# The last additions of an AdaLN transformer pair: three of eight chunks scaled by ScalarE and added by GpSimd, five by VectorE

## The chip, the cores and the metric

One core of one Trainium2 chip runs the whole program. The metric is the device time in microseconds of one launch, taken as the median of several runs. DVE is VectorE, ACT is ScalarE, POOL is GpSimd, PE is TensorE, SP is SyncE (which here only issues transfers and waits).

## What is computed

Two transformer layers with adaptive layer norm over 16 sequences of 256 tokens of width 128 (4096 tokens). Each layer has an attention part and a mixture of experts, and both add their result to the residual `x`, scaled by a gate that depends on the sequence. The change touches the very last line of this:

```python
x = L0_attn_x                                      # (16, 256, 128)
...                                                # layer 0: attention, experts
h = _layernorm(x) * (1 + ca) + sa                  # layer 1
x = x + ga * _L1_attn_ref(h, ...)
h = _layernorm(x) * (1 + cb) + sb
x = x + gb * _L1_ffn_ref(h, ...)                   # gb: one value per sequence and feature
return x
# inside _L1_ffn_ref, 7 routed experts and a shared one:
return ALPHA * top1_val[..., None] * routed + shared
```

## The kernel before

The residual lies in on-chip memory for the whole run as `X`, features on the 128 partitions and the 4096 tokens along the free axis. It is worked in eight chunks (`NCH`) of 512 tokens (`CH`), each of two sequences (`BPC`) of 256 tokens (`SEQ`).

The routed experts work on tokens sorted by expert. Each sorted tile of 128 tokens goes through PE (L677 transposes it, L686 and L693 are the two input products, L703 the output product), is weighted by ACT (L1028), and is sent back to its tokens' rows in the DRAM tensor `token_rows` by an indirect transfer that POOL issues (L1668). The last shared-expert products (L637, L639, L646) follow; DVE adds them with `add_shared`.

What is left then is the return of the routed results:

- SP, in `returned(1)` (L307 to L318), waits for all indirect transfers (L312) and issues eight loads of 256 KB, one a chunk, from `token_rows` into `N` (L316). The last of them waits for the last product that still reads its part of `N`.
- PE, in `turn_back(1, k)` (L727), waits for the load of chunk k, and from k = 2 on for DVE to have finished chunk k - 2, then transposes four 128x128 pieces into PSUM bank 6 or 7 (L734).
- DVE, in `add_routed(1, k)` (L1487), does two `gated` instructions a chunk (L1337), one for each sequence, because the gate `gab` is a column of its own for each sequence: `X = PS * gab + X`, 128x256 each.
- SP, at L325 to L328, goes through the chunks in order, waits for chunk t to be added (L326) and issues its store of 256 KB to `out` (L327), and then waits for all stores to land.

ACT and POOL have nothing to do in this stretch. ACT's queue ends with the SiLU of the last shared products, POOL's with its last `send`. The buffers `sqb` and `rsb` (four slots of 128x512 each) serve the experts in slots 0 and 1; slots 2 and 3 are free there. `va_ones` and `wo_zero` are semaphores of a few fills that POOL does at the start of the program.

Of the kernel before, what the change touches and what calls it, by code (L numbers as in the profile page):

```python
# [14 lines left out]
ALU = mybir.AluOpType  # L15
ACT = mybir.ActivationFunctionType
AX_X = mybir.AxisListType.X

P = 128
BATCH, SEQ, D = 16, 256, 128  # L20
TOK = BATCH * SEQ
CH = 512
NCH = TOK // CH
BPC = CH // SEQ
# [17 lines left out]
def adaln_kernel(nc, a):  # L42
    ctx = ExitStack()
    with ctx:
# [3 lines left out]
        def sem(name):  # L48
            return ctx.enter_context(nc.semaphore(name))


        X = sb("X", [P, TOK])
        H = sb("H", [P, TILES * ROW])
        N = sb("N", [P, TOK])
# [4 lines left out]
        ident = sb("ident", [P, P])  # L59
# [34 lines left out]
        gab = sb("gab", [P, 4, BATCH])  # L94
# [3 lines left out]
        wo1 = sb("wo1", [P, 2, D])  # L98
# [16 lines left out]
        sqb = sb("sqb", [P, 4, CH])  # L115
        rsb = sb("rsb", [P, 4, CH])
# [41 lines left out]

        PS = ctx.enter_context(nc.psum_tensor("PS", [P, 8, CH], FP32))

        C_QB, C_KB, C_OUTB, C_GA, C_BA, C_G1, C_B1, C_G2, C_B2, C_INL, C_FB2 = range(11)

        def col(n):
# [20 lines left out]
        RS = [{n: sem(f"r{l}_{n}") for n in (  # L184
            "xt", "logits", "s_gate", "onehot", "counts", "step", "pos",
            "dispatched", "s_up", "s_silu", "s_hidden", "s_sum", "s_x",
            "back", "x")} for l in range(2)]
# [4 lines left out]
        chunk_in = [sem(f"chunk_in{n}") for n in range(NCH)]  # L192
        r_fill, r_fix = sem("r_fill"), sem("r_fix")
        st_out = sem("st_out")
        va_ones, wo_zero = sem("va_ones"), sem("wo_zero")

        block = ctx.enter_context(nc.Block())

# [45 lines left out]
        def _(sp):  # L244
# [14 lines left out]
            for dst, src in ((wqkv, a["wqkv"]), (vb, a["vb"]), (qmask, a["qmask"]),  # L259
                             (ident, a["ident"]), (identb, a["identb"]), (maskqk, a["maskqk"]),  # L260
                             (maskkq, a["maskkq"])):
                sp.dma_start(dst[...], src).then_inc(ld_a, 16)
            sp.wait_ge(va_ones, 1)
            for head in range(HEADS0):
                p = 32 * (head // 4) + HD0 * (head % 2)
                sp.dma_start(wout[p:p + HD0, head % 4 // 2, :], a["wout"][head * HD0:(head + 1) * HD0, :]).then_inc(ld_a, 16)
# [6 lines left out]
            for dst, src in ((wpv[:, 0:HEADS1 * DEPTH], a["wp"]), (wpv[:, HEADS1 * DEPTH:], a["wv1"]), (bp[:, :, :], a["bp"]),  # L273
                             (prefix[:, :], a["prefix"])):
                sp.dma_start(dst, src).then_inc(ld_l1, 16)
            sp.wait_ge(wo_zero, 1)
            for head in range(HEADS1):
                p = 32 * (head % 4)
                sp.dma_start(wo1[p:p + HD1, head // 4, :], a["wo1"][head * HD1:(head + 1) * HD1, :]).then_inc(ld_l1, 16)
# [43 lines left out]
            tiles(1)  # L323
            returned(1)
            for t in range(NCH):  # L325
                sp.wait_ge(RS[1]["x"], t + 1)  # L326
                sp.dma_start(a["out"][:, t * CH:(t + 1) * CH], X[:, t * CH:(t + 1) * CH]).then_inc(st_out, 16)  # L327
            sp.wait_ge(st_out, 16 * NCH)  # L328

# [2 lines left out]
        def _(pe):  # L332
# [159 lines left out]
            for t in range(A_STEPS):  # L492
                b, u, v = t // 8, t % 8, t - A_LAG
# [233 lines left out]
            def turn_back(l, k):  # L727

                q = RS[l]
                pe.wait_ge(chunk_in[k], 16 * l + 32)  # L730
                if k >= 2:
                    pe.wait_ge(q["x"], k - 1)
                for n in range(4):
                    m = nc.tensor.transpose(PS[:, 6 + k % 2, n * P:(n + 1) * P], N[:, k * CH + n * P:k * CH + (n + 1) * P],  # L734
                                            ident[:, :])
                m.then_inc(q["back"], 1)
# [15 lines left out]
            pe.wait_ge(RS[0]["s_x"], NCH)  # L752
            ln(LN_MODA1, X, residual_ready)
            pe.wait_ge(ld_l1, LD_L1)
            pe.wait_ge(va_ones, 7)

            def project_zv(b):
                pe.wait_ge(ln_out, LNO + 8 * LN_MODA1 + b // BPC + 1)
# [94 lines left out]

            pe.wait_ge(ld_m1, 64)
            moe(dict(MOE[1], ready_pe=lambda k: pe.wait_ge(b_x, 2 * k + 2)))
            for k in range(NCH):
                turn_back(1, k)


        @block.scalar  # L860
        def _(act):
# [242 lines left out]
            invert_sums1(BATCH - 1)  # L1104

            moe(MOE[1])


        @block.vector
        def _(dve):  # L1110
# [130 lines left out]
                    dve.wait_ge(a_pj, b)  # L1241
                nc.vector.tensor_tensor(ao[:, :], av[:, :], rec[:, :], ALU.mult).then_inc(a_on, 1)

            dve.wait_ge(va_ones, 6)
            dve.wait_ge(mod_step, 10)
            for t in range(A_STEPS):
                b, u = t // 8, t % 8
# [239 lines left out]
            def add_routed(l, k):  # L1487
                dve.wait_ge(RS[l]["back"], k + 1)
                if k == NCH - 1:
                    dve.wait_ge(RS[l]["s_x"], NCH)  # L1490
                for b in range(BPC):
                    m = gated(l, k * BPC + b, PS[:, 6 + k % 2, b * SEQ:(b + 1) * SEQ])
                m.then_inc(RS[l]["x"], 1)
# [93 lines left out]

            dve.wait_ge(b_x, BATCH)
            moe(MOE[1])
            for k in range(NCH):  # L1590
                add_routed(1, k)


        @block.gpsimd
        def _(pool):
# [29 lines left out]
                                                ALU.is_ge, 0.0, base=0, channel_multiplier=-1)  # L1625
                m.then_inc(b_cut, 1)

            nc.gpsimd.memset(wo1[:, :, :], 0.0).then_inc(wo_zero, 1)
            nc.gpsimd.memset(wout[:, :, :], 0.0).then_inc(va_ones, 1)
            nc.gpsimd.memset(region[:, 0:3 * VAW], 0.0).then_inc(va_ones, 1)  # L1630
            nc.gpsimd.memset(mxs[:, :, :], 0.0).then_inc(va_ones, 1)
            pool.wait_ge(va_ones, 3)
            for n in range(3):
                nc.gpsimd.memset(region[:, n * VAW:n * VAW + 2 * HEADS0 * 32].rearrange("p (k c) -> p k c", c=32)[:, :, 24:32],
                                 1.0).then_inc(va_ones, 1)
# [20 lines left out]
            def moe(c):  # L1656
                l, q = c["l"], RS[c["l"]]
                pool.wait_ge(q["pos"], 1)
                pool.wait_ge(r_fill, 48)
                for n in range(TILES):  # L1660
                    pool.wait_ge(q["s_hidden"], n * 7 // 8 + 3 if l else min(n * 2 // 3 + 1, NCH * c["NH"] + 2 - LATE_AT[l]))
                    nc.gpsimd.indirect_dma_start(sorted_rows[l][:, :], bass.IndirectOffsetOnAxis(pos[:, n:n + 1], 0),  # L1662
                                                 rows[l][:, n, :], None).then_inc(q["dispatched"], 16)

                def send(k):
                    r = k % RING
                    pool.wait_ge(q["y"], l * SLOTS + k + 1)
                    nc.gpsimd.indirect_dma_start(  # L1668
                        token_rows[l][:, :], bass.IndirectOffsetOnAxis(slot_in[:, r, D:D + 1].bitcast(mybir.dt.int32), 0),
                        slot_out[:, k % OUTS, :], None).then_inc(q["sent"][r], 16)  # L1670

                for k in range(SLOTS_AT[l]):
                    send(k)
# [12 lines left out]
            for n in range(4 * BATCH):  # L1686
                cut1(n)
            moe(MOE[1])


# [75 lines left out]
```

## Time and profile before

| | us |
|---|---|
| median of 3 runs | 1017.04 |
| lowest and highest run | 1012.84, 1019.17 |
| the profiled execution, its own time | 1007.75 |
| its span, from the first to the last instruction | 1006.0 |
| granted TensorE clock over the span, of full speed | 0.978 |

The profile shows one execution. Its span is 1.75 us shorter than its own time, and its own time is 9.3 us (0.9%) below the median of the three timed runs. PE is busy for 93% of the span, and the chain of work that ended last runs over PE for 81% of it; DVE is busy for 62%, ACT for 55%, POOL for 46%. Positions in microseconds below are from the start of the span. The stretch that the change touches lies between 996 and 1006.

### The profile page before, as it was taken

How to read it: one execution, taken by the hardware profiler on the slowest of the kernel's cores; microseconds unless marked ns; L12 is line 12 of the kernel's file. 1: busy time of each engine (PE TensorE's matmuls, PEld its weight loads, DVE VectorE, ACT ScalarE, POOL GpSimd, SP SyncE). 2: the span in 40 equal slices, each digit the busy share in tenths (PEclk: the TensorE clock that was granted, in tenths of full speed). 3: DMA queues.
4: the chain of work that ended last, by engine and by line, in shares of the span. 5: the costliest groups of instructions: out<-in, count | busy, mean ns of one | idle time of the engine just before them, and what ended most of it. 6: DMA issues, size and time to landing. Idle time of an engine off the chain costs nothing.

```text
span 1006.0 us, 21539 instructions
## 1 busy us (share of the span) xinstructions
PE 932.9 (93%) x7391; PEld 600.5 (60%) x7391; DVE 621.9 (62%) x2056; ACT 554.8 (55%) x1075; POOL 460.2 (46%) x697
## 2 busy tenths in 40 slices
PE   8999999999989989999996798889997999999997
PEld 3566777777654223334642796456664644499995
DVE  4788888888824975872553454578772653344444
ACT  5536676766666554574521474567875622255551
POOL 1146777777741955640056464344552043323331
PEclk9999999999999997999999899999997999999999
DMA  6720000000001000031011335000000000121115
GB/s 216 240 72 13 8 13 13 10 10 13 13 20 76 0 0 1 0 121 47 1 35 45 82 96 192 13 2 1 3 1 1 1 30 29 34 61 49 50 30 178
DMA packets 38329, 45.82 MB, mean 46 GB/s; under 512 B 7840, under 2 KB 31648, under 8 KB 37360
## 3 DMA queue, kind: packets, MB, share of 16 engines
q1 hardware_dynamic: 33712, 35.13, 11.6%
q0 software_dynamic: 4512, 9.32, 2.8%
q8 instruction: 62, 1.02, 0.4%
q14 instruction: 43, 0.35, 0.1%
HBM read 31.19 MB, written 18.69 MB: 50 GB/s over the span
## 4 chain that ended last, share of the span: by engine, by line
PE 81%; ACT 6%; DVE 6%; issue 3%; POOL 2%; DMA 1%; SPq 0%; DVEq 0%; ACTq 0%; POOLq 0%
PE PS L686 5%; PE PS L703 5%; PE PS L693 5%; PE PS L444 5%; PE PS L486 5%; PE PS L340 4%; PE PS L637 4%; PE PS L639 4%; PE PS L646 4%; PE PS L457 4%; PE PS L349 3%; PE PS L546 2%; PE PS L437 2%; PE PS L813 2%; PE PS L794 2%
## 5 line engine op out<-in xcount | busy, mean ns | idle before, releaser
L922 ACT ACTIVATE pw<-PS 128x384 f32<-128x384 f32 x256 | 111.6, 488 | 71.2 <-PE PS L466 68.5
L1602 POOL TENSOR_SCALAR_AFFINE_SELECT pw<-pw 128x256 f32<-128x256 f32 x256 | 104.6, 432 | 75.3 <-ACT pw L922 73.1
L1200 DVE CUSTOM_DVE_ANT_0 PS<-PS,above 128x256 f32<-128x256 f32 x256 | 115.9, 453 | 31.4 <-PE PS L437 31.2
L1668 POOL DMA_INDIRECT token_rows<-xnb,slot_in x77 | 73.8, 958 | 104.3 <-ACT xnb L1028 104.3
L1654 POOL TENSOR_TENSOR XS<-XS,N 128x512 f32<-128x512 f32 x64 | 81.1, 1289 | 57.1 <-DVE N L1278 34.6
L444 PE MATMUL PS<-kf,qm 32*128 32x256 f32 x512 | 103.4, 426 | 0.5 <-POOL qm L1611 0.5
L1454 DVE TENSOR_TENSOR rsb<-sqb,PS 128x256 f32<-128x256 f32 (+1 forms) x77 | 42.6, 553 | 84.6 <-PE PS L693 84.0
L1202 DVE CUSTOM_DVE_ANT_0 PS<-PS,above 128x128 f32<-128x128 f32 x256 | 84.6, 330 | 0.0
L1624 POOL TENSOR_SCALAR_AFFINE_SELECT pw<-pw 128x256 f32<-128x256 f32 x128 | 55.9, 471 | 59.8 <-ACT pw L1073 59.8
L1611 POOL TENSOR_SCALAR qm<-qs,qmask 128x256 f32<-128x256 f32 x64 | 59.5, 931 | 44.7 <-ACT kf L903 44.7
L1011 ACT ACTIVATE sqb<-PS 128x512 f32<-128x512 f32 x48 | 28.7, 597 | 89.2 <-PE PS L637 89.2
L469 PE MATMUL PS<-qm,kf 32*128 32x256 f32 x512 | 76.3, 374 | 0.0
L1362 DVE TENSOR_TENSOR rsb<-sqb,PS 128x512 f32<-128x512 f32 x48 | 32.9, 687 | 70.1 <-PE PS L639 69.9
L1172 DVE TENSOR_TENSOR xnb<-PS,rsb 128x512 f32<-128x512 f32 x56 | 38.7, 691 | 58.7 <-ACT rsb L888 49.7
L1662 POOL DMA_INDIRECT sorted_rows<-H,pos x32 | 30.9, 965 | 80.7 <-DVE pos L1434 66.8
L1662 POOL DMA_INDIRECT sorted_rows<-region,pos x32 | 30.7, 959 | 80.3 <-DVE pos L1434 48.8
L686 PE MATMUL PS<-xnb,pw 128*128 128x128 f32 x460 | 64.8, 277 | 0.0
L693 PE MATMUL PS<-xnb,pw 128*128 128x128 f32 x460 | 64.4, 276 | 0.0
L970 ACT ACTIVATE PS<-PS,cols 128x512 f32<-128x512 f32 x64 | 42.2, 662 | 39.3 <-PE PS L546 24.1
L437 PE MATMUL PS<-kf,qm 32*128 32x128 f32 x512 | 62.4, 270 | 0.0
L546 PE MATMUL PS<-N,wxs 128*128 128x512 f32 x112 | 60.1, 623 | 2.0 <-DVE N L1287 0.4
L437 PEld LDWEIGHTS PS<-kf,qm 32*128 32x128 f32 x512 | 60.8, 185 | 0.8
(214 smaller groups left out, 2363.4 us busy)
## 6 DMA issues: line engine op xcount, KB each, us to landing
sorted_rows<-empty_rows_dram SPq DMA_DIRECT2D x2, 2535.0 KB, 14.7
slot_in<-sorted_rows SPq DMA_DIRECT2D x77, 65.0 KB, 1.9
N<-token_rows SPq DMA_DIRECT2D x16, 256.0 KB, 4.6
X<-xT_dram SPq DMA_DIRECT2D x8, 256.0 KB, 5.6
token_rows<-empty_rows_dram SPq DMA_DIRECT2D x1, 2048.0 KB, 24.9
ATT<-gate_dram SPq DMA_DIRECT2D x1, 2048.0 KB
XS<-down_dram SPq DMA_DIRECT2D x1, 2048.0 KB
H<-up_dram SPq DMA_DIRECT2D x1, 2048.0 KB
```

What stands on the lines that cost most here:

```text
L437: nc.tensor.matmul(PS[:, bank, SEQ:SEQ + P], qm[r, b % 3, g, 0:P], kf[r, b % 3, 0:P], start=True, stop=True).then_inc(a_s, 1)
L444: nc.tensor.matmul(PS[:, bank, 0:SEQ], qm[r, b % 3, g, P:SEQ], kf[r, b % 3, :], start=True, stop=True)
L469: m = nc.tensor.matmul(PS[:, bank, 0:SEQ], kf[r, b % 3, 0:P], qm[r, b % 3, g, :], start=False, stop=True, skip_group_check=True)
L546: nc.tensor.matmul(PS[:, k, :], wxs[:, :], V[:, s], start=False, stop=True, skip_group_check=True).then_inc(i_p, 1)
L686: m = nc.tensor.matmul(PS[:, b, n * P:(n + 1) * P], wgate[:, b, n * P:(n + 1) * P], xnb[:, b, 0:P], start=True, stop=True)
L693: m = nc.tensor.matmul(PS[:, 2 + b, n * P:(n + 1) * P], wup[:, b, n * P:(n + 1) * P], xnb[:, b, 0:P], start=True, stop=True)
L922: nc.scalar.activation(pw[:, w % 2, j + n, :], PS[:, A_PST + (2 * v + n) % 3, 0:3 * P], ACT.Exp).then_inc(a_p, 1)
L1200: nc.vector.tensor_tensor_reduce(x[:, 0:SEQ], x[:, 0:SEQ], above[:, :], 1.0, -3e38, ALU.add, ALU.max, mx[:, t // 8 % 2, 1, j, g:g + 1])
L1202: nc.vector.tensor_tensor_reduce(x[:, SEQ:SEQ + P], x[:, SEQ:SEQ + P], above[:, P:SEQ], 1.0, -3e38, ALU.add, ALU.max, mx[:, t // 8 % 2, 0, ...
L1602: m = nc.gpsimd.affine_select(x[:, :, SEQ * k:SEQ * k + P], x[:, :, SEQ * k:SEQ * k + P], [[0, 2], [1, P]], ALU.is_ge, 0.0, base=0, channe ...
L1654: nc.gpsimd.tensor_tensor(XS[:, s], XS[:, s], V[:, s], ALU.add).then_inc(i_x, 1)
L1668: nc.gpsimd.indirect_dma_start(token_rows[l][:, :], bass.IndirectOffsetOnAxis(slot_in[:, r, D:D + 1].bitcast(mybir.dt.int32), 0), slot_out ...
```

## The change

Of the eight last chunks, 1, 3 and 5 (`SCALED`) no longer go through DVE. ACT reads their transposed values from PSUM, scales them by the gate column and writes them into free slots of `sqb` and `rsb`; POOL adds them to `X`. DVE does chunks 0, 2, 4, 6 and 7 (`ADDED`) as before. PE's transposes go on in the order of the chunks, but alternate between banks 7 and 3 for the scaled ones and between banks 6 and 4 for the others, so a bank is taken again after two chunks of its own path. SP's stores stay in the order of the chunks; for a scaled chunk they wait on a new semaphore `x_added`, two counts a chunk. `add_routed(1, ...)` and `turn_back(1, ...)` are no longer called; for layer 0 both stay. At the start of the program `wo_zero` is folded into `va_ones`, whose counts move up by one.

```diff
+        SCALED, ADDED = (1, 3, 5), (0, 2, 4, 6, 7)
+        scaled = [sqb[:, 2, :], sqb[:, 3, :], rsb[:, 2, :]]
...
-        va_ones, wo_zero = sem("va_ones"), sem("wo_zero")
+        va_ones = sem("va_ones")
+        x_scaled, x_added = sem("x_scaled"), sem("x_added")
...
-            sp.wait_ge(va_ones, 1)
+            sp.wait_ge(va_ones, 2)
...
-            sp.wait_ge(wo_zero, 1)
+            sp.wait_ge(va_ones, 1)
...
             for t in range(NCH):
-                sp.wait_ge(RS[1]["x"], t + 1)
+                if t in SCALED:
+                    sp.wait_ge(x_added, 2 * SCALED.index(t) + 2)
+                else:
+                    sp.wait_ge(RS[1]["x"], ADDED.index(t) + 1)
                 sp.dma_start(a["out"][:, t * CH:(t + 1) * CH], X[:, t * CH:(t + 1) * CH]).then_inc(st_out, 16)
...
+            def turn_last(k):
+
+                pe.wait_ge(chunk_in[k], 48)
+                if k in SCALED:
+                    i, bank = SCALED.index(k), 7 if SCALED.index(k) % 2 == 0 else 3
+                    if i >= 2:
+                        pe.wait_ge(x_scaled, 2 * i - 2)
+                else:
+                    i, bank = ADDED.index(k), 6 if ADDED.index(k) % 2 == 0 else 4
+                    if i >= 2:
+                        pe.wait_ge(RS[1]["x"], i - 1)
+                for n in range(4):
+                    m = nc.tensor.transpose(PS[:, bank, n * P:(n + 1) * P], N[:, k * CH + n * P:k * CH + (n + 1) * P],
+                                            ident[:, :])
+                m.then_inc(RS[1]["back"], 1)
+
             for k in range(NCH):
-                turn_back(1, k)
+                turn_last(k)
...
             moe(MOE[1])
+            for i, k in enumerate(SCALED):
+                act.wait_ge(RS[1]["back"], k + 1)
+                for b in range(BPC):
+                    n = k * BPC + b
+                    nc.scalar.activation(scaled[i][:, b * SEQ:(b + 1) * SEQ], PS[:, 7 if i % 2 == 0 else 3, b * SEQ:(b + 1) * SEQ],
+                                         ACT.Copy, scale=gab[:, 3, n:n + 1]).then_inc(x_scaled, 1)
...
             moe(MOE[1])
-            for k in range(NCH):
-                add_routed(1, k)
+            for i, k in enumerate(ADDED):
+                dve.wait_ge(RS[1]["back"], k + 1)
+                if k == NCH - 1:
+                    dve.wait_ge(RS[1]["s_x"], NCH)
+                for b in range(BPC):
+                    m = gated(1, k * BPC + b, PS[:, 6 if i % 2 == 0 else 4, b * SEQ:(b + 1) * SEQ])
+                m.then_inc(RS[1]["x"], 1)
...
             moe(MOE[1])
+            pool.wait_ge(RS[1]["s_x"], NCH - 1)
+            for i, k in enumerate(SCALED):
+                for b in range(BPC):
+                    s = slice((k * BPC + b) * SEQ, (k * BPC + b + 1) * SEQ)
+                    pool.wait_ge(x_scaled, i * BPC + b + 1)
+                    nc.gpsimd.tensor_tensor(X[:, s], X[:, s], scaled[i][:, b * SEQ:(b + 1) * SEQ], ALU.add).then_inc(x_added, 1)
```

The waits on `va_ones` that other engines have at the start (PE's 7, DVE's 6, POOL's 3) become 8, 7 and 4.

## Rows read from the trace of the kernel before

**Rows 1.** The chain that ended last, its end: start us, us, what

```profile
996.00 1.67 DVE X L1337 x4
997.67 0.14 issue
997.81 0.64 PE PS L734 x4
...
1002.25 0.87 DVE X L1337 x2
1003.12 0.39 DVEq L44
```

**Rows 2.** Timeline, 960 to 1006: start us, us, engine line what [idle before <-releaser]

```profile
995.80 1.04 PE L734 MATMUL PS<-ident,N 128*128 128x128 f32 x8
...
996.00 7.51 DVE L1337 SCALAR_TENSOR_TENSOR X<-PS,gab,X 128x256 f32<-128x256 f32 x18 [1.22 <-PE PS L646]
```

**Rows 3.** L327, the stores: the first alone, then the last alone

```profile
L327 SPq DMA_DIRECT2D out_dram<-X x1: 350/350/350, 997.7 to 997.7; - x1
...
DMA to landing us min/median/max: 3.2/3.2/3.2
...
L327 SPq DMA_DIRECT2D out_dram<-X x1: 332/332/332, 1003.5 to 1003.5; - x1
...
DMA to landing us min/median/max: 2.0/2.0/2.0
```

**Rows 4.** L316, the loads, each alone: chunks 5, 6 and 7

```profile
L316 SPq DMA_DIRECT2D N<-token_rows x1: 518/518/518, 993.6 to 993.6; - x1
...
DMA to landing us min/median/max: 5.2/5.2/5.2
...
L316 SPq DMA_DIRECT2D N<-token_rows x1: 1187/1187/1187, 994.2 to 994.2; - x1
...
DMA to landing us min/median/max: 5.5/5.5/5.5
...
L316 SPq DMA_DIRECT2D N<-token_rows x1: 709/709/709, 995.4 to 995.4; - x1
...
DMA to landing us min/median/max: 5.0/5.0/5.0
```

**Rows 5.** Windows: length, PE, PEld, DVE, ACT, POOL busy, PEclk, DMA share, GB/s

```profile
1000.00:1001.00 1.00, 0.75 (x6) 0.42 (x4) 0.97 (x4) 0.00 (x0) 0.00 (x0) 1.00 1.05 402
...
1002.00:1003.00 1.00, 0.60 (x4) 0.36 (x4) 1.00 (x3) 0.00 (x0) 0.00 (x0) 1.00 0.99 375
1003.00:1004.00 1.00, 0.00 (x0) 0.00 (x0) 0.51 (x2) 0.00 (x0) 0.00 (x0) 1.00 0.90 344
1004.00:1005.00 1.00, 0.00 (x0) 0.00 (x0) 0.00 (x0) 0.00 (x0) 0.00 (x0) 1.00 0.94 350
```

**Rows 6.** Groups by shape: line engine op, out<-in, count | busy us, mean ns | idle

```profile
L942 ACT ACTIVATE ATT<-PS,cols 128x256 f32<-128x256 f32 x16 | 7.6, 474 | 4.3 <-PE PS L425 4.3
...
L1616 POOL TENSOR_TENSOR H<-H,ATT 128x256 f32<-128x256 f32 x16 | 11.6, 722 | 6.2 <-ACT ATT L942 6.2
```

**Rows 7.** Timeline, 430 to 446, VectorE and GpSimd: additions beside two kinds of VectorE work

```profile
436.85 1.27 POOL L1654 TENSOR_TENSOR XS<-XS,N 128x512 f32<-128x512 f32 x1 [0.45 <-DVE N L1287]
437.26 0.70 DVE L1278 SCALAR_TENSOR_TENSOR PS<-XS,PS 128x512 f32<-128x512 f32 x1 [0.49 <-ACT PS L970]
...
438.59 0.68 DVE L1293 SCALAR_TENSOR_TENSOR H<-XS,H 128x512 f32<-128x512 f32 x1
438.75 1.65 POOL L1654 TENSOR_TENSOR XS<-XS,N 128x512 f32<-128x512 f32 x1 [0.64 <-DVE N L1287]
```

**Rows 8.** The same end of layer 0: windows (as rows 5), then the timeline

```profile
628.00:630.00 2.00, 1.68 (x7) 1.25 (x7) 1.24 (x4) 0.00 (x0) 0.00 (x0) 0.50 1.04 264
...
628.72 1.09 PE L734 MATMUL PS<-ident,N 128*128 128x128 f32 x4 [0.32 <-DMA N<-token_rows]
```

More of the change, by code:

```diff
@@ L754, in _ @@
             pe.wait_ge(ld_l1, LD_L1)
-            pe.wait_ge(va_ones, 7)
+            pe.wait_ge(va_ones, 8)
             def project_zv(b):
@@ L1242, in normalise @@
                 nc.vector.tensor_tensor(ao[:, :], av[:, :], rec[:, :], ALU.mult).then_inc(a_on, 1)
-            dve.wait_ge(va_ones, 6)
+            dve.wait_ge(va_ones, 7)
             dve.wait_ge(mod_step, 10)
@@ L1626, in cut1 @@
                 m.then_inc(b_cut, 1)
-            nc.gpsimd.memset(wo1[:, :, :], 0.0).then_inc(wo_zero, 1)
+            nc.gpsimd.memset(wo1[:, :, :], 0.0).then_inc(va_ones, 1)
             nc.gpsimd.memset(wout[:, :, :], 0.0).then_inc(va_ones, 1)
@@ L1631, in _ @@
             nc.gpsimd.memset(mxs[:, :, :], 0.0).then_inc(va_ones, 1)
-            pool.wait_ge(va_ones, 3)
+            pool.wait_ge(va_ones, 4)
             for n in range(3):
```

## The prediction

> **What bounds the kernel now.** PE bounds nearly all of the span, but the change leaves that part alone, so the reading begins at its end. I read the chain that ended last first. From 996.00 on it goes back and forth between DVE's additions (L1337) and PE's transposes (L734), until DVE ends at 1003.12 + 0.39 = 1003.51 [rows 1]. The timeline then shows DVE without a pause: 18 additions fill 7.51 us, 0.417 us each [rows 2]. Two of them are the last shared ones and sixteen the routed ones, 0.83 us a chunk. So far DVE looks like the limit of this stretch, and three chunks less would be worth 3 x 0.83 = 2.5 us.
>
> The third view says otherwise. The end of the span isn't the end of DVE but the landing of the last store: it is issued at 1003.5 and lands 2.0 us later, at 1005.5, and the span ends 0.5 us after that [rows 3]. The first store, issued at 997.7, took 3.2 us and landed at 1000.9 [rows 3]. A store that needs 2.0 us by itself and takes 3.2 us stood in a queue. From the first landing to the last it is 1005.5 - 1000.9 = 4.6 us for seven more chunks, 0.66 us each. A chunk is 512 x 128 x 4 bytes = 262 KB, and at the 344 to 402 GB/s that the windows show [rows 5] it takes 0.65 to 0.76 us. The share of the transfer engines that is busy stays between 0.90 and 1.05 from 1000 to 1005 [rows 5]. So the stores already follow each other about as fast as the transfers run; DVE only keeps just ahead of them. The loads are the third term. Chunks 5, 6 and 7 are issued at 993.6, 994.2 and 995.4 and land at 998.8, 999.7 and 1000.4 [rows 4], so no engine can add chunk 7 before about 1000.5.
>
> **The change part by part.** I follow each chunk through the new order, with the landings of before.
>
> *PE.* Chunks 0 and 1 are transposed by 995.80 + 1.04 = 996.84, as before [rows 2]. Chunk 2 no longer waits for DVE, since it has bank 4. Four transposes take 0.64 us [rows 1]. With the loads and banks as they are, chunk 2 ends at about 997.4, 3 at 997.95, 4 at 998.6 (its bank is free at 997.67), 5 at 998.8 + 0.65 = 999.5, 6 at 999.7 + 0.7 = 1000.4 and 7 at 1000.4 + 0.7 = 1001.1. Nothing is queued behind these on PE.
>
> *DVE.* The two shared additions and chunk 0 end at 996.00 + 1.67 = 997.67 as before [rows 1]. Chunk 2 ends at 998.5, chunk 4 runs from 998.6 to 999.5. Then DVE waits for a load: chunk 6 from 1000.45 to 1001.3, chunk 7 to 1002.15. DVE drops six instructions, 6 x 0.417 = 2.5 us, but its end moves only from 1003.51 to 1002.15, by 1.36 us, because 0.95 us of the saving becomes a wait for the load of chunk 6 and the rest is the wait ahead of chunk 4 and rounding.
>
> *ACT.* It gets six scaled copies of 128x256 from PSUM. The nearest row, also out of PSUM and with a column as operand, has 474 ns [rows 6], 0.95 us a chunk at most. ACT scales chunk 1 from 996.9 to 997.8, chunk 3 from 998.0 to 998.9, chunk 5 from 999.6 to 1000.5. It sits idle in between. The form itself, Copy with a scale column, runs in the same part of the program (L1028), so I count no table load. If one were needed after all, it would push POOL's chain back, which has 0.4 us of slack (below).
>
> *POOL.* It gets six additions of 128x256 at 722 ns [rows 6], 4.33 us. The first can start when the first half of chunk 1 is scaled, at 997.4. Back to back they end at 998.85 (chunk 1), 1000.3 (chunk 3) and 1001.75 (chunk 5); for chunk 5 the scaled half is ready at 1000.1, so the chain never waits for ACT. The waits that stand on POOL's queue hold nothing else up, because nothing stands behind them.
>
> *SP.* Stores leave in order, and one issue takes 0.33 to 0.35 us [rows 3]. Store 0 goes at 997.7 as before, 1 waits for POOL until 998.9 (before it went some 0.8 us after store 0), 2 goes at 999.25, 3 at 1000.35, 4 at 1000.7, 5 at 1001.8, 6 at 1002.15, 7 at 1002.5. Store 2, whose data is ready at 998.5, is held for 0.75 us behind store 1; that is the price of the fixed order.
>
> *The sum.* The last issue moves from 1003.5 to 1002.5, a gain of 1.0 us at the engine side. At the transfer side the same eight chunks have to go out. The first lands at 1000.9 as before. At 0.66 us a chunk the seventh after it lands at 1000.9 + 4.6 = 1005.5; each store's own earliest landing (issue + 2.0) is checked against that: 1 at 1000.9 against 1001.6, 3 at 1002.35 against 1002.9, 5 at 1003.8 against 1004.2, 7 at 1004.5 against 1005.5. No store is late for its place in the queue, so the transfers end where they did. In the last three microseconds of before the share was 0.99, 0.90 and 0.94 [rows 5], so 0.17 us of idle time could be closed. The term I take is 0.1 us faster. Its bounds: 0.4 us faster, if the seven chunks go at the 402 GB/s of one window [rows 5] less what the loads had of it, about 0.60 us each; and 0.3 us slower, if late stores 1 and 2 leave the transfers with a hole once the loads are done.
>
> The renumbered semaphores at the start cost nothing: the same fills stand in the same order on POOL. Without that cover the wait would be one fill, well under 1 us.
>
> **May POOL and DVE add at the same time?** The rows show both answers. POOL's 128x512 addition took 1.27 us beside L1278, which reads one operand from PSUM and one from on-chip memory, and 1.65 us beside L1293, which reads two from on-chip memory [rows 7], 0.38 us more. The new neighbour, L1337, reads PSUM, `X` and a gate column, so it resembles L1278. I take 0.72 us. The other bound is an addition that each time waits out a whole DVE one, 0.72 + 0.42 = 1.14 us. By the Trainium skill (SBUF — State Buffer, "Who interferes with whom") a VectorE instruction with at most one input in SBUF, outside the two-port modes, doesn't contend with GpSimd, while one with two holds up a GpSimd instruction that reads there. The trace agrees with both halves (1.27 and 1.65 us), and by that rule the sum stays as it is.
>
> **The rivals.**
>
> *The transfers give the gain free.* If a store at the end isn't held by those before it, the last one lands 2.0 us after its issue, at 1004.5, and the kernel is 1.0 us faster. For it: the last store of before took only 2.0 us [rows 3]. Against it: that one came after a share of 0.90 [rows 5], while now stores 5, 6 and 7 come within 0.7 us. The Trainium skill (DMA: Bandwidth & Descriptors, "Anatomy of one DMA") fits one transfer at about 2.0 us plus its bytes at 436 GB/s; as an estimate by that page the last store would land 2.6 us after its issue, at 1005.1, 0.4 us faster, a result inside the forecast's own bounds. The trace differs for a store, 2.0 us with the data in it [rows 3].
>
> *POOL's chain is too slow.* Store 5 keeps its place as long as it is issued by 1005.5 - 2 x 0.66 - 2.0 = 1002.2; the sum has 1001.8. So the chain has 0.4 us of slack, and from (1002.2 - 997.4) / 6 = 0.80 us an addition on it decides. At 1.14 us for the four that run beside DVE and 0.72 us for two, POOL ends at 997.4 + 6.0 = 1003.4, stores 5 to 7 land by 1003.4 + 2.0 + 1.3 = 1006.7, and the kernel is 1.2 us slower; at 1.14 us for all six it ends at 1004.2 and the kernel is 2.0 us slower.
>
> *PE's clock halves in the new gaps.* In layer 0, where PE waited for these loads, the granted clock was 0.50 and four transposes took 1.09 us [rows 8], 0.45 us more than 0.64. Then chunk 7 is added by about 1002.7 and its store leaves at 1002.7; its place in the queue asks for 1003.5. That costs nothing.
>
> **How the numbers follow.** I give the forecast (the transfers decide, 0.4 faster to 0.3 slower) 0.60, the free gain 0.18, POOL's chain 0.22. The sum was made in the profiled execution: span 1006.0 - 0.1 = 1005.9. Added to the median of the runs shown, 1017.04 - 0.1 gives 1016.9. All cases lie between 1.0 us faster and 2.0 us slower, at most 0.2% of the kernel; about 1% is what a measurement of this kernel can tell from no change. The range is therefore that of the measurement: runs of the same kernel lay between 1012.84 and 1019.17, and the profiled one at 1007.75. With the cases at either end of the runs, 1012.84 - 1.0 = 1011.8 and 1019.17 + 2.0 = 1021.2; a median of runs seldom falls at the upper end, while one execution lay below the lower, so I take 1011.5 to 1020.5. Faster or slower by over 1% can only come from such scatter: 0.02 each.
>
> **What would show it.** The last store is issued near 1002.5 less any shift of the stretch, but takes about 3.0 us to land instead of 2.0. DVE sits idle for some 0.9 us ahead of chunk 6, released by PE and behind it the load. POOL's six additions stand back to back at 0.72 us. The share of the transfers stays near 1.0 from chunk 0's store to the end. The forecast is wrong if the last store lands 2.0 us after its issue, if POOL's additions are over 0.80 us, or if ACT loads a table.

## The result, and the profile after

| | us |
|---|---|
| changed kernel, median of 9 runs | 1022.29 (1020.55 to 1025.9) |
| kernel before, median of 9 runs | 1016.25 (1012.84 to 1019.17) |
| ratio, with its 95% interval | 1.0052 (1.0033 to 1.0071) |
| profiled execution: own time, span | 1021.06, 1019.3 |

The change costs about 5.3 us (0.0052 x 1016.25; by the interval 3.4 to 7.2). That is within 1%, as forecast, but the time lies above the range (1011.5 to 1020.5), and the loss is clear of the noise.

The spans of the two profiled executions differ by 13.3 us. To see what of that belongs to the change, a landmark is needed: the start of the last shared product (L646 before, L653 after). It is the last PE instruction that doesn't depend on the returned tokens. The rows give the first and the last start of these products, before and then after.

```profile
L646 PE MATMUL PS<-rsb,XS x64: 592/592/697, 807.2 to 995.4; 128*128 128x512 f32 x64
```

```profile
L653 PE MATMUL PS<-rsb,XS x64: 592/592/697, 813.8 to 1003.7; 128*128 128x512 f32 x64
```

Up to the landmark the profiled executions are 8.3 us apart, in code that is the same in both but for the counts of the fills at the start. From there to the end it takes 1006.0 - 995.4 = 10.6 us before and 1019.3 - 1003.7 = 15.6 us after. Only these 5.0 us match the 5.3 us of the timed runs; the 8.3 us are the scatter of single executions (the profiled one of before was itself 8.5 us under its median). They arise in layer 0, between 560 and 620 us, where PE stands idle now and then in one execution and not in the other. The windows from 580 to 600 us show it (length, then PE, PEld, DVE, ACT and POOL busy, clock, transfer share, GB/s): before, after, and the first kernel of the experiments below, whose code up to the landmark is that of the changed kernel.

```profile
580.00:600.00 20.00, 20.00 (x182) 20.00 (x181) 11.52 (x42) 14.50 (x43) 13.24 (x14) 1.00 0.36 95
```

```profile
580.00:600.00 20.00, 17.82 (x149) 16.73 (x148) 9.33 (x34) 11.47 (x35) 10.70 (x12) 1.00 0.28 78
```

```profile
580.00:600.00 20.00, 20.00 (x182) 20.00 (x181) 11.21 (x42) 14.61 (x42) 13.16 (x14) 1.00 0.36 97
```

What makes one execution take this stretch more slowly is open; the change isn't it, since the third kernel has the changed code there. All positions below with a **t** count from the landmark.

The timeline of the changed kernel shows the new order at work (start, us, engine, line, what, and in brackets the idle time before):

```profile
1005.17 0.84 ACT L1134 ACTIVATE sqb<-PS,gab 128x256 f32<-128x256 f32 x2 [3.11 <-PE PS L875]
...
1005.80 2.79 POOL L1728 TENSOR_TENSOR X<-X,sqb 128x256 f32<-128x256 f32 x4 [7.88 <-ACT sqb L1134]
1005.99 5.45 SPq L334 DMA_DIRECT2D out_dram<-X  x8
...
1007.24 0.88 DVE L1366 SCALAR_TENSOR_TENSOR X<-PS,gab,X 128x256 f32<-128x256 f32 x2 [0.50 <-PE PS L875]
...
1008.12 0.84 ACT L1134 ACTIVATE rsb<-PS,gab 128x256 f32<-128x256 f32 x2 [0.95 <-PE PS L875]
...
1008.68 1.41 POOL L1728 TENSOR_TENSOR X<-X,rsb 128x256 f32<-128x256 f32 x2
1008.94 1.66 DVE L1366 SCALAR_TENSOR_TENSOR X<-PS,gab,X 128x256 f32<-128x256 f32 x4 [0.82 <-PE PS L875]
```

The bracket after POOL's first row is its idle time between its last send and its first addition, 7.88 us. POOL's last addition ends at 1008.68 + 1.41 = 1010.09, DVE's at 1010.60. The last store is issued at t = 7.3, against 8.1 before [rows 3], and lands 2.9 us later, at 1013.9:

```profile
L334 SPq DMA_DIRECT2D out_dram<-X x1: 443/443/443, 1011.0 to 1011.0; - x1
...
DMA to landing us min/median/max: 2.9/2.9/2.9
```

So the output is complete at t = 10.2, and it was complete at t = 1005.5 - 995.4 = 10.1 before [rows 3]. Up to here nothing is gained and nothing is lost. But the program goes on for 5.4 us more, where it took 0.5 us before. The windows of this time show no engine at work, and only the end of the last store:

```profile
1013.00:1015.00 2.00, 0.00 (x0) 0.00 (x0) 0.00 (x0) 0.00 (x0) 0.00 (x0) 0.50 0.07 28
1015.00:1017.00 2.00, 0.00 (x0) 0.00 (x0) 0.00 (x0) 0.00 (x0) 0.00 (x0) 0.50 0.00 0
```

The waits of SP's queue name something at the closing line of the program (L44), put down to PE for want of a better name. Before:

```profile
SPq L44 <- DMA out_dram<-X: 1.7, 1, 1.7
...
SPq L44 <- PEq L44: 0.2, 1, 0.2
```

After:

```profile
SPq L44 <- PEq L44: 5.2, 1, 5.2
SPq L44 <- DMA out_dram<-X: 2.5, 1, 2.5
```

Asked for all instructions of line L44, the trace shows the closing barrier: each engine has a DRAIN and then signals. The drains of ACT, PE and DVE end within 0.1 us of those engines' last work (DVE's after the change at 1010.67, its work at 1010.60). POOL's doesn't. Of before:

```profile
L44 POOLq DRAIN  x1: 10175/10175/10175, 988.4 to 988.4; - x1
...
L44 DVEq DRAIN  x1: 914/914/914, 1002.7 to 1002.7; - x1
...
L44 SPq DRAIN  x1: 7/7/7, 1005.8 to 1005.8; - x1
```

Of after:

```profile
L44 POOLq EVENT_SEMAPHORE  x2: 17/17/17, 1019.1 to 1019.2; - x2
...
L44 PEldq DRAIN  x1: 700/700/700, 1009.0 to 1009.0; - x1
L44 POOLq DRAIN  x1: 10082/10082/10082, 1009.0 to 1009.0; - x1
...
L44 SPq DRAIN  x1: 7/7/7, 1014.1 to 1014.1; - x1
```

POOL's drain is recorded from the time when nothing else is left on its queue, while its last instructions still run, and takes 10 us. Before, it ended at 998.6, 9.0 us after POOL's last send (989.6); the additions and stores went on until 1005.5 beside it, so it cost nothing. After, it ends at 1019.08, again 9.0 us after POOL's last instruction (1010.09), and now only the closing signals come after it. So POOL's queue didn't end with its last send, nor did POOL have nothing to do in this stretch, as was taken ahead of the prediction: its drain stood behind the send.

### The profile page after: what moved, and what is told of

Read it like the earlier page. It is cut to its first block, busy times and chain, and to the rows that moved or that the text cites. A ratio compares the mean times of both kernels' runs of the same rounds, so it can differ in the third digit from the quotient of the medians.

```text
span 1019.3 us, 21544 instructions
## 1 busy us (share of the span) xinstructions
PE 934.6 (92%) x7391; PEld 601.0 (59%) x7391; DVE 619.3 (61%) x2050; ACT 555.9 (55%) x1081; POOL 465.7 (46%) x703
## 3 DMA queue, kind: packets, MB, share of 16 engines
q1 hardware_dynamic: 33712, 35.13, 11.3%
## 4 chain that ended last, share of the span: by engine, by line
PE 78%; ACT 6%; DVE 6%; issue 4%; DMA 2%; POOL 2%; SPq 1%; DVEq 0%; ACTq 0%; POOLq 0%
PE PS L710 6%; PE PS L451 5%; PE PS L493 5%; PE PS L693 5%; PE PS L700 5%; PE PS L347 4%; PE PS L464 4%; PE PS L644 3%; PE PS L646 3%; PE PS L653 3%; PE PS L356 3%; PE PS L553 2%; PE PS L444 2%; PE PS L820 2%; PE PS L801 2%
## 5 line engine op out<-in xcount | busy, mean ns | idle before, releaser
L693 PE MATMUL PS<-xnb,pw 128*128 128x128 f32 x460 | 65.9, 281 | 0.0
L700 PE MATMUL PS<-xnb,pw 128*128 128x128 f32 x460 | 65.6, 280 | 0.0
L1044 ACT ACTIVATE sqb<-PS 128x256 f32<-128x256 f32 (+1 forms) x77 | 37.6, 488 | 45.4 <-PE PS L693 42.5
```

The source lines that it names most:

```text
L693: m = nc.tensor.matmul(PS[:, b, n * P:(n + 1) * P], wgate[:, b, n * P:(n + 1) * P], xnb[:, b, 0:P], start=True, stop=True)
L700: m = nc.tensor.matmul(PS[:, 2 + b, n * P:(n + 1) * P], wup[:, b, n * P:(n + 1) * P], xnb[:, b, 0:P], start=True, stop=True)
```

## The experiments

Two theories stood against each other: **D**, the closing drain on POOL takes 9.0 us after POOL's last instruction and decides; **U**, the loss arises ahead of the last stretch, where the two profiles differ by 8.3 us. The first four kernels share one set of runs of the kernel before (median 1005.87 us). The timed runs tell a kernel from that one; to compare a kernel with the changed one, the stretch from the landmark to the end of the profiled execution is used, 10.6 us before and 15.6 us in the changed kernel.

**The changed kernel without POOL's closing drain.**

```diff
-        block = ctx.enter_context(nc.Block())
+        block = ctx.enter_context(nc.Block(no_gpsimd_drain=True))
```

> The changed kernel, but the closing barrier of the program is one that doesn't drain POOL (Block(no_gpsimd_drain=True)). Theory D (drain): in both profiles POOL's closing drain ends 9.0 us after POOL's last instruction (989.6 to 998.6 before, hidden behind the additions; 1010.1 to 1019.1 after, the last thing that runs), and the 5.2 us between the landing of the last store (1013.9) and the end (1019.3) are this drain. Then this kernel ends about 0.5 us after its last store has landed, the stretch from the end of the last shared product (PE L653) to the end shrinks from 15.0 us to 9.9, and the median falls by about 5 us, to that of the kernel before within 1 us. Theory U (upstream): the two profiles also differ by 8.3 us ahead of this stretch, so the loss arises there (the renumbered fills, the code's place); then the median stays near 1022.

Measured: 1004.53 us, ratio to before 0.999 (0.997 to 1.001). The landmark is at 993.6 and the span 1004.4, so the last stretch takes 10.8 us, 4.8 us less than in the changed kernel. (The expectation counted from the end of the last product, 0.6 us later: 9.9 us forecast, 10.2 measured.) SP's wait at the end is gone:

```profile
SPq L44 <- DMA out_dram<-X: 2.6, 1, 2.6
...
SPq L44 <- PEq L44: 0.2, 1, 0.2
```

The whole loss goes with the drain, and U falls: the code ahead of the landmark is still that of the changed kernel, and the time is that of before.

**The kernel before with one late POOL instruction.**

```diff
             moe(MOE[1])
+            pool.wait_ge(RS[1]["x"], NCH)
+            nc.gpsimd.memset(qmask[:, :], 0.0)
```

> The kernel before, with one more instruction: POOL waits until DVE has added all eight chunks and then fills the 128x4 tile qmask, which nobody reads any more. No ScalarE or GpSimd share of the additions. Theory D: POOL's last instruction now ends at about 1003.6 + 0.1 of the old time scale, the drain 9.0 us later at 1012.7, the end at 1012.9 instead of 1006.0: the kernel is 6.5 to 7 us slower for an instruction of 0.1 us. Theory U: nothing changes by more than 1 us.

Measured: 1011.71 us, ratio 1.0054 (1.0029 to 1.0078). The fill takes 0.10 us and ends at 1002.61; the drain's row says 1002.5 + 9.10 = 1011.6, 9.0 us after it.

```profile
L44 POOLq DRAIN  x1: 9103/9103/9103, 1002.5 to 1002.5; - x1
```

The stretch after the landmark is 17.5 us instead of 10.6, 6.9 us more. The timed difference is 0.0054 x 1005.87 = 5.4 us, with an interval of 2.9 to 7.8 us that holds the 6.9. One fill of 0.1 us, with none of the change, costs as much as the change does.

**The changed kernel with a drain ahead of POOL's additions.**

```diff
             pool.wait_ge(RS[1]["s_x"], NCH - 1)
+            nc.gpsimd.drain()
             for i, k in enumerate(SCALED):
```

> The changed kernel with an explicit drain on POOL between its last sent tile and its first addition. If the 9 us are paid once, for indirect transfers that POOL has issued since the last drain (D1), the first drain takes 9 us where POOL is nearly idle (989.6 to 998.6 of the old time scale, 1.2 us later than its first addition would start) and the closing one is short: the end comes about 4 to 5 us earlier than in the changed kernel. If every drain costs 9 us once indirect transfers are in the program (D2), the closing drain is 9.0 us again, and the kernel is 0.5 to 1.5 us slower than the changed one.

Measured: 1006.9 us, ratio 1.0015 (0.999 to 1.0041). First the explicit drain (L1724), then the closing one:

```profile
L1724 POOLq DRAIN  x1: 10178/10178/10178, 990.0 to 990.0; - x1
```

```profile
L44 POOLq DRAIN  x1: 2224/2224/2224, 1002.3 to 1002.3; - x1
...
L44 SPq DRAIN  x1: 7/7/7, 1008.1 to 1008.1; - x1
```

The closing drain ends at 1004.52, 0.07 us after POOL's last addition (1004.45). So the 9 us are paid once, and a second drain with no indirect transfer in between is free. The early drain ends at 1000.2; the landmark is at 997.0, so that is t = 3.2, where the additions began at t = 2.1 in the changed kernel. The end comes 11.3 us after the landmark, 4.3 us earlier than in the changed kernel. By the timed runs alone this kernel is told neither from the one before nor clearly from the changed one (1.0015, up to 1.0041, for 1.0052, down to 1.0033); the drain rows and the last stretch decide here.

**DVE adds the scaled chunks.**

```diff
                 m.then_inc(RS[1]["x"], 1)
+                if k + 1 in SCALED:
+                    j = SCALED.index(k + 1)
+                    for b in range(BPC):
+                        ...
+                        dve.wait_ge(x_scaled, j * BPC + b + 1)
+                        nc.vector.tensor_tensor(X[:, s], X[:, s], scaled[j][...], ALU.add).then_inc(x_added, 1)
...
-            pool.wait_ge(RS[1]["s_x"], NCH - 1)
-            for i, k in enumerate(SCALED):
-                ...
-                    nc.gpsimd.tensor_tensor(X[:, s], X[:, s], scaled[i][...], ALU.add).then_inc(x_added, 1)
```

> The changed kernel with the same banks, order of stores and ScalarE scaling, but DVE instead of POOL adds the scaled chunks 1, 3 and 5 from on-chip memory. POOL ends with its last sent tile. Theory D: POOL's drain is hidden again and the median falls by 4 to 6 us against the changed kernel, although DVE has as many additions as before. Theory U, and the rival that ScalarE's part is what costs: no change within 1 us. DVE's additions of two on-chip operands should take 0.43 to 0.5 us each.

Measured: 1005.93 us, ratio 0.999 (0.9971 to 1.001). The last stretch is 10.8 us, the drain is hidden again (it ends at 997.7), and the last store leaves at t = 7.4. DVE's additions took less than expected: two of them 0.75 us.

```profile
995.12 1.66 DVE L1366 SCALAR_TENSOR_TENSOR X<-PS,gab,X 128x256 f32<-128x256 f32 x4 [1.22 <-PE PS L653]
996.69 0.75 DVE L1631 TENSOR_TENSOR X<-X,sqb 128x256 f32<-128x256 f32 x2
997.36 0.87 DVE L1366 SCALAR_TENSOR_TENSOR X<-PS,gab,X 128x256 f32<-128x256 f32 x2
...
1000.27 1.65 DVE L1366 SCALAR_TENSOR_TENSOR X<-PS,gab,X 128x256 f32<-128x256 f32 x4
```

DVE does as many additions here as before and still the last store leaves 0.7 us earlier (t = 7.4 for 8.1). From the first row to the last DVE takes 1001.92 - 995.12 = 6.80 us, for 7.51 before [rows 2]. A scaled chunk takes it 0.67 us from start to start (996.69 to 997.36) instead of 0.83, which gives 3 x 0.16 = 0.5 us. The twelve gated instructions take the other 4.8 us, 0.2 us less than at 0.417 us each; that they no longer wait in turn with PE for two banks is the likely reason, but no run here separates it. ScalarE's part costs nothing, and POOL's additions aren't needed for what the change gains in issue time.

**A drain between the layers.**

```diff
             pool.wait_ge(RS[0]["s_x"], NCH)
+            nc.gpsimd.drain()
             nc.gpsimd.memset(va1[:, :, :, :, HD1:], 1.0).then_inc(va_ones, 1)
```

> The changed kernel with an explicit drain on POOL between the two layers, after layer 0's last sent tile and before POOL's fill of va1, where POOL has about 10 us of idle time. POOL issues 141 indirect transfers in all: 32 + 39 in layer 0, 32 + 38 in layer 1. Theory C (count): a drain costs a share for each indirect transfer since the last drain, 9.0 us / 141 = 0.064 us. Then the middle drain takes 71 x 0.064 = 4.5 us in idle time, and the closing one ends 70 x 0.064 = 4.5 us after POOL's last addition: the end comes about 4.5 us earlier than in the changed kernel and within 0.5 us of the landing of the last store. Theory F (fixed): a drain costs 9 us if any indirect transfer went before it; then the closing one is 9.0 us again and the end is that of the changed kernel.

Measured: 1010.66 us beside 1007.42 for before, ratio 1.0028 (1.0006 to 1.005). The middle drain, then the closing one:

```profile
L1712 POOLq DRAIN  x1: 5872/5872/5872, 624.9 to 624.9; - x1
```

```profile
L44 POOLq DRAIN  x1: 6884/6884/6884, 1001.6 to 1001.6; - x1
```

The middle drain took 5.9 us after 71 indirect transfers, the closing one ended 5.8 us after POOL's last addition, with 70 since the middle one. Neither theory fits: it isn't fixed at 9.0, and it isn't 4.5. The 5.9 us count from the middle drain's own start; POOL had been waiting for 4.7 us by then, since its last send (620.2). From 70 to 141 transfers the time grows by 3.2 us, 0.045 us each; if it grows evenly, 2.6 us are left over at none, and those aren't there when no transfer was issued (0.07 us above). The end comes 12.6 us after the landmark, 3.0 us better than the changed kernel and 2.0 us worse than before; the timed difference of 2.8 us (0.6 to 5.0) agrees.

**Kernels without the layers.** To see what the length of the drain hangs on, eight small kernels leave out both transformer layers: they load `x`, issue indirect transfers on POOL, do eight additions of 128x256 on POOL, and store. Each was profiled once. The table's last column is the time from the end of the last addition to the end of the closing drain. The loop of e7 (N is 141; in e6 it is 12):

```python
for n in range(N):
    nc.gpsimd.indirect_dma_start(token_rows[1][:, :], bass.IndirectOffsetOnAxis(token_ids[:, n % TILES:n % TILES + 1], 0),
                                 V[:, 0:D], None).then_inc(credit, 16)
    pool.wait_ge(credit, 16 * (n + 1))
```

| kernel | transfers, semaphores, waits | us |
|---|---|---|
| e11 | none | 0.1 |
| e6 | 12, one semaphore, POOL waits for each | 1.1 |
| e7 | 141, the same | 2.4 |
| e10 | 141, the same, in groups of 32 | 2.4 |
| e9 | 141, twelve semaphores | 3.3 |
| e13 | 128 to four tensors, one semaphore, POOL and SP wait | 1.3 |
| e14 | 128 to four tensors, one semaphore, SP waits | 1.3 |
| e15 | 128 to four tensors, twelve semaphores, SP waits | 2.2 |

Two of them as rows, the additions and then the drain: e11, where 10.5 + 4.63 = 15.1 is 0.1 us after 10.43 + 4.60, and e7, where 363.9 + 7.01 = 370.9 is 2.4 us after 363.95 + 4.60.

```profile
10.43 4.60 POOL L268 TENSOR_TENSOR X<-X 128x256 f32<-128x256 f32 x8
...
L44 POOLq DRAIN  x1: 4629/4629/4629, 10.5 to 10.5; - x1
```

```profile
363.95 4.60 POOL L268 TENSOR_TENSOR X<-X 128x256 f32<-128x256 f32 x8 [1.33 <-DMA token_rows<-N,token_ids]
...
L44 POOLq DRAIN  x1: 7008/7008/7008, 363.9 to 363.9; - x1
```

> The kernel without the layers and without any indirect transfer. All theories: the closing drain ends 0.1 to 0.3 us after POOL's last addition. With 12 transfers it was 1.1 us and with 141 it was 2.4; if it is over 0.8 us here, the closing drain has a price of its own.

> A kernel that leaves out both transformer layers: it loads x, lets POOL issue 12 indirect transfers of 128 rows one after the other, each waited for, then does eight additions on POOL and stores x. Theory C: the closing drain ends 12 x 0.064 = 0.8 us after POOL's last addition. Theory F: 9 us after it.

> The same kernel without the layers, with 141 indirect transfers instead of 12. Theories C and F both say that the closing drain ends 9.0 us after POOL's last addition; if it doesn't, the 9 us hang on something else than the number of indirect transfers, as the gathering of rows in other tensors.

> The kernel without the layers, 141 indirect transfers each waited for, but on twelve semaphores in turn instead of one. The closing drain took 2.4 us after POOL's last addition with one semaphore, 1.1 us with 12 transfers on one. If the number of semaphores is what the full program's 9.0 us hang on (theory S), it rises here to over 5 us; if not, it stays at 2.4 us within 0.3.

> The kernel without the layers, 141 indirect transfers on one semaphore, but issued back to back in groups of 32 with a wait only after each group, as layer 0's dispatch does. If the drain's time hangs on transfers that were under way together (theory O), it rises well over 2.4 us; if only on their number, it stays at 2.4 us within 0.3.

> The kernel without the layers: 128 indirect transfers, 32 to each of the four DRAM tensors of the full program, on one semaphore, issued back to back; POOL and SP both wait for all of them. Theory W (who waits): a drain is short for transfers that POOL has itself waited for, so it takes 2.2 to 2.6 us after POOL's last addition, as with 141 to one tensor. Theory T (tensors): over 4 us.

> The same, but POOL doesn't wait for the transfers; SP does, and POOL goes on after a later load of SP's has landed. Theory W: the drain takes much longer than in the run where POOL waits, over 4 us. Otherwise it is the same within 0.3 us.

> The same as the run before, with twelve semaphores in turn instead of one. From the pair measured so far (2.4 us on one, 3.3 us on twelve) it adds 1.0 us. Together with W it should come near the 9.0 us of the full program.

What follows: without indirect transfers the drain is free, with any of them it isn't. Twelve semaphores instead of one add 0.9 us both times (2.4 to 3.3 and 1.3 to 2.2), too little for theory S. Issue in groups (O) and the engine that waits (W) change nothing (2.4 and 2.4, 1.3 and 1.3). Four tensors instead of one (T) don't lengthen the drain. But 128 transfers to four tensors took 1.3 us where 2.2 to 2.6 were expected, 1.1 us less than 141 to one; number, tensors and the pause ahead of the additions (3.0 for 1.3 us) all differ between the two, so that step is unexplained. Nor does the number explain it evenly: 12 transfers already cost 1.1 us. None of them reaches the 9.0 us of the full program; 141 transfers on twelve semaphores give only 3.3, and the expectations for e7 (9.0) and e15 (near 9.0) both failed.

**The changed kernel with POOL's own waits.** The last attempt at the length, in the full program:

```diff
             pool.wait_ge(RS[1]["s_x"], NCH - 1)
+            for l in range(2):
+                pool.wait_ge(RS[l]["dispatched"], 16 * TILES)
+            for r in range(RING):
+                pool.wait_ge(r_sent[r], 16 * sum(n[r] for n in LOADS_AT))
```

> The changed kernel, with POOL waiting for all of its indirect transfers itself ahead of its first addition (two dispatch and twelve send semaphores). They have landed 6 us before that addition, so the waits are free. Theory W: the closing drain falls from 9.0 to 3.5 us or less and the end comes about 5 us earlier, as without a drain. If W is wrong, the kernel takes the time of the changed one, 5 us more than before.

Measured: 1023.88 us beside 1019.9, ratio 1.0039 (1.0021 to 1.0058). The drain ends 9.0 us after the last addition, as in the changed kernel, and the last stretch is 15.5 us. W is wrong here too: the transfers had all landed and POOL had seen it, and the drain took its 9.0 us all the same. That the runs of one kernel before differ by 14 us from set to set (1005.87 and 1019.9) shows again that only kernels of one set are to be compared.

**Half of each store.** Is it the transfers that keep the gain away once the drain is gone? Both kernels with half of the output left out:

```diff
-                sp.dma_start(a["out"][:, t * CH:(t + 1) * CH], X[:, t * CH:(t + 1) * CH]).then_inc(st_out, 16)
+                sp.dma_start(a["out"][:, t * CH:t * CH + CH // 2], X[:, t * CH:t * CH + CH // 2]).then_inc(st_out, 16)
```

> The changed kernel without POOL's closing drain, and each store writes only the first 256 of its 512 columns, so half of the output is left out and half of the store's bytes are gone. This tests whether the transfers take the gain of the additions. In the profile of the changed kernel without the drain the last store was issued 7.2 us after the start of the last L653 product and the end came 10.8 us after it. If the transfers bound the end, the last store now lands about 1.8 us after its issue and the end comes 9.3 to 9.6 us after the last product's start. If the issue bound it, the end stays within 0.4 us of 10.8.

> The kernel before, each store writing only the first 256 of its 512 columns (half of the output is left out). The same cut in the changed kernel without POOL's drain moved the end from 10.8 to 9.7 us after the start of the last shared product. If the additions on DVE bound the end here once the transfers are relieved, the last store is still issued 8.1 us after that product's start and the end comes at 10.2 to 10.4 us; the difference to 9.7, 0.5 to 0.7 us, is all that moving the three chunks could give with half the bytes.

Measured in the changed kernel without the drain: landmark 997.9, span 1007.6, so 9.7 us; the last store leaves at t = 7.3, as in the changed kernel.

```profile
L334 SPq DMA_DIRECT2D out_dram<-X x1: 443/443/443, 1005.2 to 1005.2; - x1
...
DMA to landing us min/median/max: 1.9/1.9/1.9
```

With whole stores, in the changed kernel without the drain, the last store took 3.1 us to land:

```profile
L334 SPq DMA_DIRECT2D out_dram<-X x1: 455/455/455, 1000.8 to 1000.8; - x1
...
DMA to landing us min/median/max: 3.1/3.1/3.1
```

Measured in the kernel before: landmark 995.6, span 1005.9, 10.3 us, the last store at t = 8.1.

```profile
L327 SPq DMA_DIRECT2D out_dram<-X x1: 333/333/333, 1003.7 to 1003.7; - x1
...
DMA to landing us min/median/max: 1.7/1.7/1.7
```

With half the bytes the changed order ends 1.1 us earlier (10.8 to 9.7), the old one only 0.3 us (10.6 to 10.3). In the old order half the bytes shorten the last store by 0.3 us (2.0 to 1.7 [rows 3]), which is the whole gain: its issue, and so the additions, bound the end. In the changed order they shorten it by 1.2 us (3.1 to 1.9): there the last store had stood behind the others, and the transfers bound the end. With whole stores the two bounds all but coincide, landings at t = 10.1 and 10.2, and that is why 0.8 us of earlier issue gives nothing. With half the bytes the changed order is 0.6 us ahead (9.7 for 10.3), inside the 0.5 to 0.7 us expected. Each is one profile; the terms are 0.1 us exact at best.

## Why the prediction was right and where it wasn't

**The step that failed** is the one on POOL's queue: "The waits that stand on POOL's queue hold nothing else up, because nothing stands behind them." One thing stood behind them, the closing drain. Its row was in the trace of before, 10.2 us long from 988.4, and it ended 7 us ahead of the last landing, so it didn't show. The forecast priced six additions at 722 ns and let POOL end at 1001.75. It should have gone on: 1001.75 + 9.0 = 1010.75, 0.3 us for the closing signals, so a span of about 1011 instead of 1006, 5 us slower. The prediction asked what covers the fills at the start, but not what POOL's own queue still holds after 989.6; it took the idle time from there to the end as free, and put the drain at nothing without a reason.

**The rival that came nearest** (1.2 to 2.0 us slower through POOL's chain) had the right engine and the wrong reason. Its test was an addition above 0.80 us; they followed each other every 2.79 / 4 = 0.70 us, and the chain ended on time.

**POOL and DVE side by side** was right. POOL's additions took no longer beside L1366 (0.70 us from one to the next, 1.41 us for two) than the 722 ns of [rows 6]; the bound of 1.14 us each wasn't touched. ACT's scaled copies took 0.84 us for two, under the 0.95 us allowed, with no table load among them.

**The rival of PE's clock** fell too: the granted clock was 1.00 from 1004 to 1011, and four transposes took 0.66 us for the 0.64 of the sum.

```profile
1007.43 0.66 PE L875 MATMUL PS<-ident,N 128*128 128x128 f32 x4 [0.23 <-DMA N<-token_rows]
```

**The additions** came out close. DVE's end was forecast at t = 1002.15 - 995.4 = 6.75 and came at 6.9; POOL's at 6.35, and came at 6.4; the last issue at 7.1, and came at 7.3. The wait ahead of chunk 6 was 0.82 us for 0.95. One small miss: DVE waited 0.50 us ahead of chunk 4 too, where the forecast had 0.1, since the loads of chunks 2 to 7 landed 0.2 to 0.3 us later after the landmark.

**The transfers** were right, and they are the reason why nothing was gained. The last landing was forecast 0.1 us earlier than before and was 0.1 us later (t = 10.2 for 10.1); the last store took 2.9 us to land for "about 3.0". Without the drain the kernel is the same as before, 0.999 (0.997 to 1.001); a forecast of 0.1 us faster is too small for the timed runs to confirm or refute. The first rival, which had the transfers give the gain free, falls by the same row. The prediction's estimate of 2.6 us for that store rests on a fit that the Trainium skill (DMA: Bandwidth & Descriptors, "Anatomy of one DMA") gives for transfers on GpSimd's path, while SP issued this one; it was 0.3 us short of the 2.9 us measured. And the bound of 0.4 us faster doesn't follow from its source: at 402 GB/s a chunk takes 0.65 us, as the prediction says itself further up, not 0.60. Nothing hung on either.

**The renumbered fills** cost nothing: up to 365 us into the program the changed kernel's PE work lies at most 0.7 us ahead of that of before, and the two kernels of the changed order without the late drain take the time of before.

**The range** was that of single runs of one kernel, with 2 us for the change on either side. It left out 1022.29 because the change's own term was 5 us and not the 2 us that it allowed at most.

No version beat the kernel before. The nearest, without the drain or with DVE's additions, is the same within 0.3%.

## What to carry to other kernels

Before work is put on an engine that is idle at the end of a program, look at the closing line in the trace: what that engine still has to do there is finished only some time after its last instruction. On POOL, in this program with 141 indirect transfers, that was 9 us, and idle time there was worth nothing until it had been paid. If POOL must work late, drain it in an earlier idle stretch (with an explicit drain ahead of its additions the closing one fell to 0.07 us). Or close the program without its drain, where all its transfers are waited for elsewhere, as SP does here; no run here tests that in another program. And ask of the last stretch whether the transfers can take an earlier issue at all: eight stores in a row gave none of 0.8 us back.

## What the runs showed of the hardware

The closing drain on POOL ended 9.0 us after POOL's last instruction in six full kernels (8.94 to 8.99 us by the rows, whose starts are rounded to 0.1 us), and so did the first drain of the kernel with an early one, whatever that instruction was: a send, an addition or a fill of 0.1 us. It was 9.0 us alike where the drain came right behind the last send, as before the change, and where 7.88 us of idle time and six additions lay between, as after it. The Trainium skill (VectorE: DVE Perf Modes, "The DRAIN you can't avoid") describes the drains around a program as constant, about 12 ns on all five engines. On SP the trace agrees (7 ns), and on ACT, PE and DVE where they have no work, in the small kernels (8 to 10 ns). On POOL it doesn't: the row has 10,082 ns, 9.0 us of them after POOL's last instruction.

It depends on indirect transfers since the last drain: 0.1 us with none, 5.8 us with 70, 9.0 us with 141 in the full program, but only 1.1 to 3.3 us with 12 to 141 of them in the small ones. A share goes with the number of semaphores (0.9 us for eleven more). What makes up the other 5.7 us of the full program is open. Not tried were other sources and index patterns, and the full program's hundreds of other POOL instructions between the transfers; a drain in mid-program comes between those as well as between the transfers.

The chain of waits doesn't show any of this. In the changed kernel its last piece is DVE at 1010.20, 9 us before the end of the span, since drains and signals aren't counted as work.

```profile
1009.81 0.39 DVEq L44
1010.20 0.39 DVE X L1366
```

An end of the chain well short of the span is the sign to read the closing line.
